# Expert results stored to places of their own and folded at the end, half of the shared tiles moved behind the expert steps

## The chip, the cores and the metric

One core of one Trainium2 chip runs one launch. The metric is device microseconds of that launch, the median of several runs. Names used: PE (TensorE), DVE (VectorE), ACT (ScalarE), POOL (GpSimd), SP (SyncE, here a queue that issues DMAs).

## The reference, cut to what matters

One transformer layer on 2048 tokens of 256 elements, float32. The second half is a mixture of experts with a shared expert:

```python
w, idx = _router(xf, rg_w, ru_w, extra_scale, extra_bias)     # top 4 of 16 experts per token
coeff = jnp.einsum('tk,tke->te', w, jax.nn.one_hot(idx, E, dtype=w.dtype))
def step(y, ew):
    wg, wu, wd, c = ew
    h = jax.nn.silu(xf @ wg.T) * (xf @ wu.T)                    # wg, wu: 176 x 256
    return (y + h @ wd.T * c[:, None], None)
y, _ = lax.scan(step, y0, (Wg, Wu, Wd, coeff.T))
z = jax.nn.silu(xf @ Sg.T) * (xf @ Su.T) @ Sd.T                 # shared expert, 352 wide
x = x + gb * (y + z)
```

## The kernel before

Three stages, each a block of its own with a barrier behind it: the projections with layernorm, sliding-window attention with routing, and the experts. Every matrix product is made of three float32r products of high and low parts (`three`, L109). Tokens are handled in 16 tiles of 128.

In the attention stage POOL's `weights` (L827) writes each token's 16 expert coefficients and its token number behind its row in `h2` (HW = 273 columns), and `dispatch` (L838) scatters the row to the four experts' regions of `xs_scr` in memory. The last pairs of tiles are dispatched behind the last attention work.

The expert stage is `experts_and_output` (L1208). Its first part runs the 16 shared tiles: per tile PE does gate and up (12 matmuls into both GU banks), the transposition XT of the tile after next, the shared down of two tiles before (YP) and the transposition HT of one tile before. PE's next gate and up waits for DVE's `gating` of this tile (L1557), which waits for ACT's `gate` (L1389). In the same tiles the 16 experts' weights are split, one a tile: ACT writes the high parts (`split_hi`, L1402), DVE the low part of gate and up (L1605, 128x704) and POOL the low part of down (L1470, 88x512). DVE also makes the table that says which rows and which expert each step has (L1508 to L1545), in tiles 0 to 3, in line with its work on the tiles; tile 5 on PE turns the table into a row. DVE adds the residual (`add_x1`) and SP stores each tile to out_x. POOL writes 128 neutral rows behind each expert's region (L1468).

The second part runs 80 steps of one expert and 128 gathered rows each, with gate and up (6 matmuls), XT of the step after next (2), down (6) of two steps before and HT (2) of one before. SP loads the rows four steps ahead (`load_x`, L1306), DVE scales the result by coefficient and gate (`y_gate`, L1569) into one of eight buffers (y_st and h2), and POOL adds it into out_x by an indirect DMA with an add in memory (L1488). The rows of one expert are different tokens, those of two experts may be the same: so `let_add` (L1316) on SP, in line with the loads, waits at an expert's first step until all adds before have landed, reading the count from the table, and lets POOL go on by `turn`.

Of the kernel before, what the change touches and what calls it, by code (L numbers as in the profile page):

```python
# [12 lines left out]
P = 128  # L13
# [31 lines left out]
SPARE = 5 * P  # L45
# [106 lines left out]
def project_qkv(nc, A, T, ctx, own):  # L152
# [87 lines left out]
    def _(eng):  # L240
# [18 lines left out]
        eng.dma_start(T["pad"][:, :], A["pad"]).then_inc(z_st, 16)  # L259
# [27 lines left out]
        eng.wait_ge(z_st, 32)  # L287
# [268 lines left out]
def attention_and_routing(nc, A, T, ctx, own):  # L556
# [41 lines left out]
    r_sm = sb("r_sm", [P, 3, 2])  # L598
    top8 = sb("top8", [P, 2, 8])
# [202 lines left out]
    def _(eng):  # L802
# [405 lines left out]
def experts_and_output(nc, A, T, out, ctx, own):  # L1208
# [18 lines left out]
    xs = T["xs_scr"]  # L1227
    NS = STEPS_RUN


    gu_hi = sb("gu_hi", [P, NE, W_GU], F32R)
# [5 lines left out]
    steps_c = sb("steps_c", [P, 4 + NE])  # L1237
    tab = sb("tab", [P, 8, NE])
    col = sb("col", [P, 8])
    entry_c = sb("entry_c", [P, 4])  # L1240
    pad_i = sb("pad_i", [P, NE], I32)
    step_i = sb("step_i", [1, 4, P], I32)
# [33 lines left out]
    x1_ld, o_out, added, turn = sems("x1_ld", 4), sems("o_out", 4), sems("added", 2), sem("turn")  # L1276
# [21 lines left out]

    @block.sync
    def _(eng):  # L1300
        def load_h2(n):
            if n >= 4:
                eng.wait_ge(xt_mm, n - 3)
            eng.dma_start(x_st[:, n % 4, 0:D], T["h2_scr"][n]).then_inc(xs_ld[n % 4], 16)

        def load_x(s, t):  # L1306

            eng.wait_ge(xt_mm, TILES + s - 3)
# [7 lines left out]
        def let_add(s):  # L1316

            for p in range(2):
                eng.wait_ge(added[p], step_entry(eng, 2 + p, s, 32 + 16 * NS))
                plain(eng)  # L1320
            eng.nop(nofuse=True).then_inc(turn, 1)  # L1321

        def load_x1(n):

            if n >= 4:
                eng.wait_ge(o_out[n % 4], 32 * (n // 4))
            eng.dma_start(y_st[:, n % 4, :], T["x1_scr"][n]).then_inc(x1_ld[n % 4], 16)

        def store_out(n):
            eng.wait_ge(y_out, n + 1)  # L1330
            for c in range(2):
                eng.dma_start(out[0:S_LEN, :].rearrange("(c n q) d -> n c q d", c=2, n=TILES)[n, c],
                              y_st[c * CH:(c + 1) * CH, n % 4, :]).then_inc(o_out[n % 4], 16)

        for n in range(2):
            load_h2(n)
        eng.dma_start(sgu_raw[:, :, :, :], A["sgu"]).then_inc(sgu_ld, 16)
        eng.dma_start(sdn_raw[:, :, :], A["sd"]).then_inc(sdn_ld, 16)
        for n in range(2, 4):
            load_h2(n)  # L1340
# [3 lines left out]
        for n in range(TILES):  # L1344
            if n < TILES - 4:
                load_h2(n + 4)
            else:
                if n == TILES - 4:
# [5 lines left out]
                load_x(n - (TILES - 4), n - (TILES - 4))  # L1354
            if n < TILES - 1:
                load_x1(n + 1)
            if n >= 2:
                store_out(n - 2)

        def step(s, r, i, first, last):  # L1360
            if runs(s, 0, NS - 5):
                load_x(s + 4, r % 4)
            if isinstance(s, int) and s < 2:
                store_out(TILES - 2 + s)
            if runs(s, 4):
                let_add(s - 4)

        for_steps(eng, step, NS)
        for s in range(NS - 4, NS):
            let_add(s)  # L1370
        for p in range(2):
            eng.wait_ge(added[p], 32 + 16 * (NS // 2))
# [4 lines left out]
    def _(eng):  # L1377
# [35 lines left out]
        for n in range(TILES):  # L1413
            gate(n, n % 2, GU[0], SH_I)
            x_hi(n + 2, n % 2)
            if n == 1:
# [5 lines left out]
            if n == 0:  # L1422
                eng.wait_ge(T["w_first"], 32 * FIRST)
            if n == FIRST:
                eng.wait_ge(w_rest, 64)
            split_hi(n)
# [417 lines left out]
```

## Time and profile before

| | |
|---|---|
| runs | 728.52, 722.45, 728.35 us; median 728.35 |
| profiled execution | 725.86 us, span 724.2 us |
| PE busy / weight loads / DVE / ACT / POOL | 77% / 72% / 55% / 39% / 41% |
| mean granted TensorE clock | 0.852 |
| shared tiles on PE | 403.8 to 486.75 us |
| first POOL subtract (L1470) | 409.8 us |
| expert steps on PE | 486.75 to 708.7 us |

A busy share is an average over stages with different limits; what a change in one stage is worth is read in that stage: what PE waits for, and what releases it. "idle before <-releaser" tells how long an engine stood before an instruction and what let it go. The clock is given as a share of 2.4 GHz: 1.00 or 0.50 when it does not change in a stretch.

### The profile page before, as it was taken

The page shows a single profiled execution, that of the slowest core. Times are in us where ns is not written, and L with a number is a line of the kernel's source. Part 1 is how long each engine was busy: PE and PEld are TensorE (multiplying, and loading weights), DVE is VectorE, ACT ScalarE, POOL GpSimd, SP SyncE. Part 2 cuts the span into 40 slices and gives each one's busy share as a digit, 9 for nine tenths or more (in the row PEclk, how much of TensorE's full clock was granted, in tenths as well). Part 3 has the DMA queues.
Part 4 walks back from the last instruction along what each step waited for, and adds up shares of the span by engine and source line. Part 5 has one row for each costly group of instructions (what it writes and reads, how often), then busy time and mean ns, then how long its engine had stood idle before and what let it go on. Part 6 is the DMA issues. An engine that isn't in the chain of part 4 may idle for free. (4 is left out here: it accounts for less than half of the span.)

```text
span 724.2 us, 14774 instructions
## 1 busy us (share of the span) xinstructions
PE 558.6 (77%) x3655; PEld 522.5 (72%) x3656; DVE 396.3 (55%) x1142; ACT 279.9 (39%) x739; POOL 300.5 (41%) x275
## 2 busy tenths in 40 slices
PE   2578841999988989889821489679895798789992
PEld 1378841898988989889720479679795697679892
DVE  3796420225456565575761677755673476357571
ACT  1334422224533343343310446354553354245450
POOL 3644405001014433352675334431463475465675
PEclk9799985559979889798955799899999999699997
DMA  7146694038835635531224936233463575476674
GB/s 209 39 138 193 172 263 124 11 110 207 197 80 148 163 100 144 145 110 62 92 99 169 320 94 187 66 85 72 83 109 66 84 127 88 67 119 103 105 113 51
DMA packets 73466, 88.93 MB, mean 123 GB/s; under 512 B 10122, under 2 KB 63369, under 8 KB 73345
## 3 DMA queue, kind: packets, MB, share of 16 engines
q1 hardware_dynamic: 53723, 58.93, 30.2%
q0 software_dynamic: 15712, 22.89, 17.5%
q10 hardware_dynamic: 3974, 6.47, 2.8%
q8 instruction: 21, 0.34, 0.2%
q14 instruction: 36, 0.29, 0.2%
HBM read 49.55 MB, written 39.66 MB: 123 GB/s over the span
## 5 line engine op out<-in xcount | busy, mean ns | idle before, releaser
L148 POOL DMA_INDIRECT xs_scr<-h,slot_u x64 | 62.4, 974 | 79.7 <-DVE slot_u L995 30.4
L113 PE MATMUL GU<-gu_hi,xT 128*128 x320 | 88.3, 359 | 4.7 <-POOL lo L1470 4.2
L1488 POOL DMA_INDIRECT out_x<-y_st,ids_st x40 | 62.3, 1558 | 66.3 <-SPq L1321 31.1
L1090 PE MATMUL O<-raw,prob 128*128 128x99 f32 (+1 forms) x512 | 80.8, 314 | 0.0
L1488 POOL DMA_INDIRECT out_x<-h,ids_st x40 | 62.2, 1554 | 40.6 <-issue 15.3
L760 ACT ACTIVATE prob<-TB 128x512 f32<-128x512 f32 x64 | 38.1, 596 | 103.3 <-PE TB L1080 76.8
L1090 PEld LDWEIGHTS O<-raw,prob 128*128 128x128 f32 x512 | 76.2, 229 | 0.4
L113 PE MATMUL YP<-dn_hi,aT 88*128 x320 | 70.1, 312 | 2.8 <-DVE aT L1554 2.5
L1630 PE MATMUL XT<-ident,x_st 128*128 128x128 f32 x192 | 40.2, 293 | 38.3 <-DMA x_st<-xs_scr 25.2
L1561 DVE TENSOR_TENSOR h_act<-GU,g_act 128x176 f32<-128x176 f32 (+1 forms) x96 | 35.7, 372 | 60.8 <-ACT g_act L1393 53.2
L1400 ACT ACTIVATE aT<-HT 88x256 fp32r<-88x256 f32 (+1 forms) x96 | 39.8, 415 | 75.4 <-PE HT L1640 69.1
L878 DVE TENSOR_REDUCE neg_m<-SB 128x4 f32<-128x512 f32 x64 | 43.0, 689 | 44.8 <-PE SB L1068 39.7
L1549 DVE TENSOR_TENSOR xT<-XT,xT 128x256 fp32r<-128x256 f32 x96 | 40.6, 423 | 40.8 <-ACT xT L1387 39.9
L1065 PE MATMUL SB<-mask_key,mask_qry 126*128 126x512 f32 x64 | 34.6, 541 | 35.7 <-POOL Q L811 24.3
L1630 PEld LDWEIGHTS XT<-ident,x_st 128*128 128x128 f32 x192 | 26.1, 147 | 47.5 <-DMA x_st<-xs_scr 31.2
L113 PEld LDWEIGHTS GU<-gu_hi,xT 128*128 128x128 f32 x320 | 55.2, 200 | 6.0 <-issue 5.9
L113 PEld LDWEIGHTS YP<-dn_hi,aT 88*128 88x128 f32 x320 | 50.4, 196 | 7.2 <-issue 4.1
L113 PE MATMUL GU<-lo,xT 128*128 x160 | 54.1, 338 | 0.0
L1387 ACT ACTIVATE xT<-XT 128x256 fp32r<-128x256 f32 x96 | 36.7, 382 | 44.8 <-PE XT L1630 43.6
L113 PE MATMUL GU<-sgu_hl,xT 128*128 128x352 f32 x192 | 37.7, 349 | 18.2 <-DVE h_act L1561 10.5
L1554 DVE TENSOR_TENSOR aT<-HT,aT 88x256 fp32r<-88x256 f32 (+1 forms) x96 | 44.5, 465 | 12.9 <-ACT aT L1400 9.4
L1393 ACT ACTIVATE g_act<-GU 128x176 f32<-128x176 f32 (+1 forms) x96 | 32.7, 341 | 46.3 <-PE GU L113 39.3
(192 smaller groups left out, 1270.1 us busy)
## 6 DMA issues: line engine op xcount, KB each, us to landing
x_st<-xs_scr SPq DMA_DIRECT2D x80, 136.5 KB, 2.3
K<-k_scr SPq DMA_DIRECT2D x48, 192.0 KB, 3.6
k_scr<-k_ev SPq DMA_DIRECT2D x8, 768.0 KB, 5.6
QC<-q_scr SPq DMA_DIRECT2D x24, 256.0 KB, 6.8
q_scr<-q_ev SPq DMA_DIRECT2D x8, 512.0 KB, 3.3
raw<-in_egu SPq DMA_DIRECT2D x8, 352.0 KB
raw<-in_egu ACTq DMA_DIRECT2D x2, 1408.0 KB
raw<-in_x SPq DMA_DIRECT2D x36, 64.0 KB, 3.0
```

What stands on the lines that cost most here:

```text
L113: mm = eng.matmul(out, a, b, start=(i + j == 0), stop=(i == len(pairs) - 1 and j == 2))
L148: eng.indirect_dma_start(T["xs_scr"], bass.IndirectOffsetOnAxis(ap=T["slot_u"][:, par, t % 2, k:k + 1], axis=0), T["h2"][:, t, :], None).t ...
L760: eng.activation(prob[:, q, :], TB[q % 2][:, :], ACT.Exp, scale=SCALE).then_inc(exp_done, 1)
L878: eng.tensor_reduce(neg_m[:, p2, 4 * q:4 * q + 4], SB[q % 2][:, :].rearrange("p (h x) -> p h x", h=4), AX.X, ALU.max, negate=True).then_in ...
L1090: mm = eng.matmul(O[:, head // 8, at:at + WIDE * VC], prob[:, q, hh * P:(hh + 1) * P], VW[:, bass.ds(HEADS * n + head, WIDE), :].rearrange ...
L1387: eng.activation(xT[:, p2, 0, :, :], XT[p2][:, 0:D].rearrange("p (k x) -> p k x", k=KD), ACT.Copy).then_inc(xT_hi2, 1)
L1400: eng.activation(aT[:, p2, 0, 0:k, :], HT[p2][0:FH, 0:k * P].rearrange("p (k x) -> p k x", k=k), ACT.Copy).then_inc(aT_hi, 1)
L1488: eng.indirect_dma_start(out, bass.IndirectOffsetOnAxis(ap=ids_st[:, r:r + 1].bitcast(U32), axis=0), results(r % 8), None, compute_op=ALU. ...
L1549: eng.tensor_tensor(xT[:, p2, 1, :, :], XT[p2][:, 0:D].rearrange("p (k x) -> p k x", k=KD), xT[:, p2, 0, :, :].bitcast(F32), ALU.subtract) ...
L1554: eng.tensor_tensor(aT[:, p2, 1, 0:k, :], HT[p2][0:FH, 0:k * P].rearrange("p (k x) -> p k x", k=k), aT[:, p2, 0, 0:k, :].bitcast(F32), ALU ...
L1561: eng.tensor_tensor(h_act[:, p2, 0:width], up, g_act[:, p2, 0:width], ALU.mult).then_inc(gated, 1)
L1630: mm = eng.transpose(XT[t % 2][:, k * P:(k + 1) * P], x_st[:, t, k * P:(k + 1) * P], ident[:, :])
```

## The change

- Routing: POOL's `weights` also works out for each chosen expert the place 4 x token + k, k being the rank of the expert among the token's four, and writes 16 such places behind the coefficients. HW is 288. Five more operations, and RP_OPS is 9.
- The first part runs 8 shared tiles (EARLY) and splits two experts a tile. ACT splits both, DVE subtracts the gate and up part of the even one, POOL that of the odd one and both down parts. Their sum with the residual goes back to `x1_scr`, not to out_x.
- The neutral rows are written by SP (`fill_up`), from an input array, in tile 3, with places of their own. The column with the expert's first step leaves the table.
- Steps: the result goes by an indirect DMA without an add to `ys_scr`, each row at its place. `let_add` and `turn` are gone. POOL waits, every second step, for sends of the step group before (`sent`).
- Behind the 80 steps the other 8 shared tiles run. Behind the last step's gate and up, `to_add`, `four` and `halves` lie where `gu_hi` lay: SP loads the 16 tiles of `x1_scr`, waits for all sends and loads `four`, a token's four results in 4 KB, two DMAs of 64 partitions a tile, six tiles ahead. POOL adds four into two and two into one, at most two tiles ahead of `final`. DVE adds the shared results of the late tiles (`add_late`) and then the fold (`finish`): tiles 0 to 3 among the late tiles, 4 to 15 behind the last shared result. SP stores to out_x.

```diff
 W_GU, W_DN = KD * 2 * FI, 2 * D
-TB_PAD, TB_COL = 9, 24
+TB_PAD, TB_COL = 9, 20
 L1_OPS, L2_OPS = 16, 16
-R_OPS, P_OPS, RP_OPS = 20, 4, 4
+R_OPS, P_OPS, RP_OPS = 20, 4, 9
 W_EXP = W_GU + W_DN
-HW = D + NE + 1
+HW = D + 2 * NE
...
+            k_of = [onehot[:, par, :, k, :] for k in range(TOPK)]
             eng.wait_ge(r_dve, R_OPS * g + R_OPS)
             c.mark(eng.tensor_tensor(rw[:, 0], rt[:, 7, :, :], esc[:, 0:1, :].broadcast_to([P, 2, NE]), ALU.mult)).wait(True)
             c.mark(eng.tensor_scalar(rw[:, 1], rw[:, 0], 1.0, None, ALU.add)).wait()
-            c.mark(eng.tensor_tensor(h2[:, 2 * par:2 * par + 2, D:IDS], mask_e[:, par].bitcast(F32), rw[:, 1], ALU.mult)).wait(True)
-            c.mark(eng.tensor_copy(h2[:, 2 * par:2 * par + 2, IDS:HW].rearrange("p a o -> p (a o)").bitcast(U32), T["ids"][:, bass.ds(n, 2)]))
+            c.mark(eng.tensor_tensor(h2[:, 2 * par:2 * par + 2, D:IDS], mask_e[:, par].bitcast(F32), rw[:, 1], ALU.mult))
+            c.mark(eng.tensor_tensor(pl[:, 0], k_of[1], k_of[3], ALU.add))
+            c.mark(eng.tensor_tensor(pl[:, 1], k_of[2], k_of[3], ALU.add)).wait(True)
+            c.mark(eng.tensor_tensor(pl[:, 2], pl[:, 0], T["ids"][:, bass.ds(n, 2)].unsqueeze(2).broadcast_to([P, 2, NE]), ALU.add)).wait()
+            c.mark(eng.tensor_tensor(pl[:, 0], pl[:, 2], pl[:, 1], ALU.add)).wait(True)
+            c.mark(eng.tensor_tensor(pl[:, 2], pl[:, 0], pl[:, 1], ALU.add)).wait(True)
+            c.mark(eng.tensor_copy(h2[:, 2 * par:2 * par + 2, IDS:HW].bitcast(U32), pl[:, 2]))
             assert c.k == RP_OPS
...
-        def let_add(s):
-
-            for p in range(2):
-                eng.wait_ge(added[p], step_entry(eng, 2 + p, s, 32 + 16 * NS))
-                plain(eng)
-            eng.nop(nofuse=True).then_inc(turn, 1)
...
+        def store_z(n):
...
+            eng.dma_start(T["x1_scr"][n], y_st[:, n % 4, :]).then_inc(z_out[n % 4], 16)
+
+        def fill_up():
+
+            eng.wait_ge(tb, TB_PAD)
+            for e in range(NE):
+                row = eng.value_load(pad_i[0:1, e:e + 1])
+                row = nc.s_assert_within(row, 0, NE * CAP, skip_runtime_bounds_check_because="a count of at most 2048 rows")
+                eng.dma_start(xs[bass.ds(row, P), :], A["pads"][e * P:(e + 1) * P, :]).then_inc(pad_st, 16)
...
+            if n == EARLY - 5:
+                fill_up()
...
-            if runs(s, 4):
-                let_add(s - 4)
+                store_z(EARLY - 2 + s)
...
+        eng.wait_ge(gu_mm, LATE)
+        for q in (2, 3, 0, 1):
+            if q == 0:
+                for t in range(4):
+                    eng.wait_ge(z_out[t], 16 * (EARLY // 4))
+            at = slice(4 * q, 4 * q + 4)
+            eng.dma_start(to_add[:, at, :], T["x1_scr"][at].rearrange("n p d -> p n d")).then_inc(add_ld[q], 16)
+            if q == 3:
+                for n in (EARLY + 4, EARLY + 5):
+                    load_h2(NS + n, n)
         for p in range(2):
-            eng.wait_ge(added[p], 32 + 16 * (NS // 2))
+            eng.wait_ge(sent[p], 32 + 16 * (NS // 2))
+
+        def load_four(n):
+            if n >= 6:
+                eng.wait_ge(folded, n - 5)
+            for c in range(2):
+                eng.dma_start(four[c * CH:(c + 1) * CH, n % 6].rearrange("p k d -> p (k d)"),
+                              halves_of(ys[0:PLACES, :].rearrange("(s k) d -> s (k d)", k=TOPK), n)[c]).then_inc(four_ld[n % 6], 16)
+
+        def store_out(n):
+            eng.wait_ge(final, n + 1)
+            for c in range(2):
+                eng.dma_start(halves_of(out, n)[c], y_st[c * CH:(c + 1) * CH, n % 4, :]).then_inc(o_out[n % 4], 16)
+
+        for n in range(6):
+            load_four(n)
+        for n in (EARLY + 6, EARLY + 7):
+            load_h2(NS + n, n)
+        for n in range(TILES):
+            store_out(n)
+            if n + 6 < TILES:
+                load_four(n + 6)
...
+        def dn_low(e):
             eng.wait_ge(w_hi2, 2 * e + 2)
             eng.tensor_tensor(lo[0:FH, e, W_GU:W_EXP], raw[0:FH, e, W_GU:W_EXP],
                               dn_hi[:, e, :].bitcast(F32), ALU.subtract).then_inc(dn_lo, 1)
 
-        eng.wait_ge(step_tab, 1)
-        for t in range(4):
-            eng.wait_ge(o_out[t], 32 * (TILES // 4))
+        for n in range(EARLY):
+            dn_low(2 * n)
+            eng.wait_ge(w_hi2, 4 * n + 3)
+            eng.tensor_tensor(lo[:, 2 * n + 1, 0:W_GU], raw[:, 2 * n + 1, 0:W_GU], gu_hi[:, 2 * n + 1, :].bitcast(F32),
+                              ALU.subtract).then_inc(dn_lo, 1)
+            dn_low(2 * n + 1)
+
         for p in range(2):
-            eng.wait_ge(added[p], 32)
+            eng.wait_ge(sent[p], 32)
 
         def step(s, r, i, first, last):
             q = r // 2 % 2
-            eng.wait_ge(turn, s + 1)
+            if r % 2 == 0 and runs(s, 4):
+
+                eng.wait_ge(sent[q], 32 * i + 32)
+                plain(eng)
+            eng.wait_ge(y_out, EARLY + s + 1)
             plain(eng)
-            if r % 2 == 0 and runs(s, 4):
-
-                eng.wait_ge(added[q], 32 * i + 32)
-            eng.wait_ge(y_out, TILES + s + 1)
-            plain(eng)
-            eng.indirect_dma_start(out, bass.IndirectOffsetOnAxis(ap=ids_st[:, r:r + 1].bitcast(U32), axis=0), results(r % 8), None,
-                                   compute_op=ALU.add).then_inc(added[q], 16)
+            eng.indirect_dma_start(ys, bass.IndirectOffsetOnAxis(ap=ids_st[:, r:r + 1].bitcast(U32), axis=0), results(r % 8),
+                                   None).then_inc(sent[q], 16)
 
         for_steps(eng, step, NS)
...
+        for n in range(TILES):
+            two = halves[:, n % 2]
+            eng.wait_ge(four_ld[n % 6], 32 * (n // 6) + 32)
+            if n >= 2:
+                eng.wait_ge(final, n - 1)
+            eng.tensor_tensor(two, four[:, n % 6, 0:2, :], four[:, n % 6, 2:4, :], ALU.add).then_inc(folded, 1)
+            eng.wait_ge(folded, n + 1)
+            eng.tensor_tensor(two[:, 0, :], two[:, 0, :], two[:, 1, :], ALU.add).then_inc(summed, 1)
...
+        def add_late(n):
+
+            eng.wait_ge(y_mm, NS + n + 1)
+            eng.wait_ge(add_ld[n // 4], 16)
+            eng.tensor_tensor(to_add[:, n, :], YP[n % 2][:, 0:D], to_add[:, n, :], ALU.add).then_inc(y_out, 1)
+
+        def finish(n):
+
+            eng.wait_ge(summed, n + 1)
+            if n < EARLY:
+                eng.wait_ge(add_ld[n // 4], 16)
+            elif n == EARLY:
+                eng.wait_ge(y_out, NS + TILES)
+            if n >= 4:
+                eng.wait_ge(o_out[n % 4], 32 * (n // 4))
+            eng.tensor_tensor(y_st[:, n % 4, :], halves[:, n % 2, 0, :], to_add[:, n, :], ALU.add).then_inc(final, 1)
...
+        for n in range(EARLY, TILES):
+            p2 = n % 2
+            gating(NS + n, p2, GU[1][:, 0:SH_I], SH_I)
+            if n < TILES - 2:
+                x_lo(NS + n + 2, p2)
+            if n < EARLY + 2:
+                s = NS + n - EARLY - 2
+                y_gate(s, s % UNROLL, s // 4)
+            else:
+                add_late(n - 2)
+            a_lo(NS + n - 1, 1 - p2, 2 if n == EARLY else 4)
+            for m in ((), (0,), (1,), (2, 3))[max(n - EARLY - 4, 0)]:
+                finish(m)
+        add_late(TILES - 2)
+        a_lo(NS + TILES - 1, 1, 4)
+        add_late(TILES - 1)
+        for n in range(4, TILES):
+            finish(n)
 
...
+        for n in range(EARLY, TILES):
+            w, p2 = NS + n, n % 2
+            shared_gate_up(w, p2)
+            if n < TILES - 2:
+                transpose_x(w + 2, (n + 2) % 4, (w + 2) // 4 + 1)
+            if n < EARLY + 2:
+                down(w - 2, p2, load_entry(w - 2 - EARLY))
+            else:
+                shared_down(w - 2, p2)
+            transpose_a(w - 1, 1 - p2, 2 if n == EARLY else 4)
+        transpose_a(NS + TILES - 1, 1, 4)
+        for w in (NS + TILES - 2, NS + TILES - 1):
+            shared_down(w, w % 2)
 
 
```

## Rows read from the trace of the kernel before

**Rows 1.** Windows: us, busy us of each engine (instructions), granted clock, DMA share, GB/s.
```profile
680.00:700.00 20.00, 20.00 (x146) 19.08 (x145) 14.52 (x37) 11.63 (x46) 14.82 (x10) 1.00 0.80 129
...
396.00:400.00 4.00, 0.69 (x2) 0.29 (x2) 0.42 (x1) 0.38 (x1) 3.08 (x4) 0.50 1.02 396
```

**Rows 2.** Waits of SP from 486 to 724: waited for, us in total, times, longest.
```profile
SPq L59 <- DMA out_x<-y_st,ids_st: 25.1, 9, 4.0
SPq L59 <- DMA out_x<-h,ids_st: 19.9, 7, 3.1
SPq L1374 <- DMA out_x<-h,ids_st: 11.8, 1, 11.8
```

**Rows 3.** Waits of PE from 486 to 724.
```profile
PE XT L1630 <- DMA x_st<-xs_scr: 25.2, 15, 3.0
```

**Rows 4.** Timeline of POOL: start, us, instruction, idle before and its releaser.
```profile
672.94 1.55 POOL L1488 DMA_INDIRECT out_x<-y_st,ids_st  x1 [3.59 <-DVE h L1577]
...
692.42 1.55 POOL L1488 DMA_INDIRECT out_x<-y_st,ids_st  x1 [0.47 <-issue]
```

**Rows 5.** Timeline of PE, gate and up of shared tiles and of steps 0 and 2.
```profile
446.65 2.16 PE L113 MATMUL GU<-sgu_hl,xT 128*128 128x352 f32 x12
...
450.64 2.17 PE L113 MATMUL GU<-sgu_hl,xT 128*128 128x352 f32 x12
...
460.37 3.86 PE L113 MATMUL GU<-sgu_hl,xT 128*128 128x352 f32 x12 [5.48 <-DVE h_act L1561]
...
466.37 2.17 PE L113 MATMUL GU<-sgu_hl,xT 128*128 128x352 f32 x12
...
486.75 0.95 PE L113 MATMUL GU<-gu_hi,xT 128*128 x2 [4.15 <-POOL lo L1470]
...
495.51 0.57 PE L113 MATMUL GU<-gu_hi,xT 128*128 x2
```

**Rows 6.** Timeline of POOL at the end of the attention stage.
```profile
371.49 0.19 POOL L835 COPY h<-ids 128x2 uint32<-128x2 uint32 x1
373.18 1.05 POOL L148 DMA_INDIRECT xs_scr<-h,slot_u  x1 [1.50 <-DVE slot_u L995]
...
384.31 0.19 POOL L835 COPY h<-ids 128x2 uint32<-128x2 uint32 x1
```

**Rows 7.** Timeline of ACT in a shared tile: the two splits.
```profile
447.43 0.78 ACT L1403 ACTIVATE gu_hi<-raw 128x704 fp32r<-128x704 f32 x1
448.11 0.62 ACT L1404 ACTIVATE dn_hi<-raw 88x512 fp32r<-88x512 f32 x1
```

**Rows 8.** A group (mean ns), and one line's min/median/max ns.
```profile
L819 POOL TENSOR_TENSOR h2t<-xn,mod 128x512 f32<-128x512 f32 x8 | 10.2, 1270 | 46.3 <-ACT xn L731 45.7 <-issue 0.6
...
L1605 DVE TENSOR_TENSOR lo<-raw,gu_hi x16: 874/892/7553, 412.8 to 483.9; 128x704 fp32r<-128x704 f32 x16
```

**Rows 9.** Timeline of POOL and of DVE in the shared tiles.
```profile
410.45 0.90 DVE L1510 TENSOR_TENSOR first_use<-count,steps_c 128x256 f32<-128x256 f32 x1 [1.32 <-DMA steps_c<-in_steps]
...
451.60 7.43 POOL L1470 TENSOR_TENSOR lo<-raw,dn_hi 88x512 fp32r<-88x512 f32 x6
...
452.23 7.55 DVE L1605 TENSOR_TENSOR lo<-raw,gu_hi 128x704 fp32r<-128x704 f32 x1
```

**Rows 10.** SP: the chain in order of time, and the timeline of SP's issues.
```profile
576.18 0.34 SPq L1314
576.66 0.27 SPq L1289
...
452.06 1.11 SPq L1332 DMA_DIRECT2D out_x<-y_st  x2
```

**Rows 11.** DMA issues: count, KB each, median us to landing.
```profile
x_st<-xs_scr SPq DMA_DIRECT2D x80, 136.5 KB, 2.3
...
xs_scr<-pad POOLq DMA_DIRECT2D x16, 136.5 KB, 2.9
...
out_x<-y_st SPq DMA_DIRECT2D x32, 64.0 KB, 2.1
```

More of the change, by code:

```diff
@@ L286, in _ @@
         eng.wait_ge(qk0_ld, 5 * LD)
-        eng.wait_ge(z_st, 32)
+        eng.wait_ge(z_st, 16)
     @block.scalar
@@ L1226, in experts_and_output @@
     ident, iota_e, count, gb, raw, lo, h2 = [T[x] for x in ("ident", "iota_e", "count", "gb", "raw", "lo", "h2")]
-    xs = T["xs_scr"]
+    xs, ys = T["xs_scr"], T["ys_scr"]
     NS = STEPS_RUN
+    LATE = NS + EARLY
+    with ExitStack() as last_use:
+        last = last_use.enter_context(nc.sbuf_tensor("last_use", [P, NE * W_GU], F32))
+    four = last[:, 0:6 * TOPK * D].rearrange("p (c k d) -> p c k d", c=6, k=TOPK)
+    to_add = last[:, 6 * TOPK * D:6 * TOPK * D + TILES * D].rearrange("p (n d) -> p n d", n=TILES)
+    halves = last[:, 6 * TOPK * D + TILES * D:6 * TOPK * D + TILES * D + 4 * D].rearrange("p (c k d) -> p c k d", c=2, k=2)
     gu_hi = sb("gu_hi", [P, NE, W_GU], F32R)
@@ L1275, in experts_and_output @@
     y_mm, y_out, picked = sem("y_mm"), sem("y_out"), sem("picked")
-    x1_ld, o_out, added, turn = sems("x1_ld", 4), sems("o_out", 4), sems("added", 2), sem("turn")
+    x1_ld, z_out, sent = sems("x1_ld", 4), sems("z_out", 4), sems("sent", 2)
+    four_ld, add_ld, folded, summed, final = sems("four_ld", 6), sems("add_ld", 4), sem("folded"), sem("summed"), sem("final")
+    o_out = sems("o_out", 4)
     block = ctx.enter_context(nc.Block())
@@ L1411, in _ @@
         eng.activation(sdn_hl[:, :, 0, :], sdn_raw[:, :, :], ACT.Copy).then_inc(sh_hi, 1)
-        for n in range(TILES):
+        for n in range(EARLY):
             gate(n, n % 2, GU[0], SH_I)
             x_hi(n + 2, n % 2)
+            if n == 0:
+                eng.wait_ge(T["w_first"], 32 * FIRST)
+            if 2 * n == FIRST:
+                eng.wait_ge(w_rest, 64)
+            split_hi(2 * n)
             if n == 1:
@@ L1454, in _ @@
             send_rows(eng, T, t, (GROUPS - 1) % 2)
-        half = P // 2
         for p in range(2):
-            eng.dma_start(out[S_LEN + p * half:S_LEN + (p + 1) * half, :], T["pad"][p * half:(p + 1) * half, 0:D]).then_inc(added[p], 16)
-            first = 2 * P * p
-            eng.dma_start(out[S_LEN + P + first:S_LEN + 3 * P + first, :], A["spare"][first:first + 2 * P, 0:D]).then_inc(added[p], 16)
-        for e in range(NE):
-            if e == 5:
-                eng.wait_ge(tb, TB_PAD)
-                with eng.Fori(0, NE // 4) as i:
-                    for j in range(4):
-                        row = eng.value_load(pad_i[0:1, bass.ds(4 * i + j, 1)], min_val=0, max_val=NE * CAP)
-                        eng.dma_start(xs[bass.ds(row, P), :], T["pad"][:, :]).then_inc(pad_st, 16)
+            for k in range(2):
+                first = PLACES + NE * P + (2 * p + k) * P
+                eng.dma_start(ys[first:first + P, :], A["pads"][0:P, 0:D]).then_inc(sent[p], 16)
+        def dn_low(e):
             eng.wait_ge(w_hi2, 2 * e + 2)
@@ L1525, in experts_of_steps @@
             c.mark(eng.tensor_scalar(row(5), cum, part, None, ALU.is_le)).wait()
-            c.mark(eng.tensor_reduce(col[:, 0:1], row(5), AX.X, ALU.add))
-            c.mark(eng.tensor_scalar(row(6), before, part, None, ALU.is_equal)).wait()
-            c.mark(eng.tensor_reduce(col[:, 1:2], row(6), AX.X, ALU.add))
+            c.mark(eng.tensor_reduce(col[:, 0:1], row(5), AX.X, ALU.add)).wait()
             c.mark(eng.tensor_scalar(row(7), e_row, col[:, 0:1], None, ALU.is_equal)).wait()
@@ L1590, in _ @@
                           ALU.subtract).then_inc(sh_lo, 1)
-        for n in range(TILES):
+        for n in range(EARLY):
             p2 = n % 2
-            if n == 5:
+            if n == EARLY // 2:
                 keep_steps()
```

149 lines of the change are left out of this document (70 added, 79 removed).

## Prediction

> **What bounds the kernel now.** I read the span in slices, then the last stage by PE's and SP's waits, by POOL's timeline and by windows, and last the stretch where the shared tiles run. The 80 expert steps run from 486.75 to about 708.7, which is 222 us or 2.78 a step. Undisturbed, a step is PE's: from 680 to 700 PE is busy throughout at full clock with 146 matmuls, 16 a step, so 2.19 us [rows 1]. The reader should see where the other 45 us go. SP stands 45.0 us in L59's table reads waiting for adds into out_x to land [rows 2]; SP is the engine that loads x_st, so PE stands 25.2 us for x_st [rows 3] and falls to half clock after some of the stops. POOL's timeline has two spacings: about 2.0 us inside an expert (0.47 idle, 1.55 issue), 5.1 at a change of expert (3.59 idle) [rows 4]. There are 15 such changes. So the steps are bound by PE plus the ordering of adds.
>
> The 16 shared tiles take 403.8 to 486.75. PE's period is 3.99 us (446.65 to 450.64), 6.0 at half clock (460.37 to 466.37) [rows 5]. Two stops matter: PE's 5.48 us before 460.37, and 4.15 before the first step, on POOL's last subtract.
>
> **The change, part by part** (times by the profiled execution, 724.2 span, 725.86 its own time, 1.7 around it; the median of the runs, 728.35, is 0.3% above that).
>
> *Routing, RP_OPS 4 to 9.* Five more operations on 32 columns, 0.25 each plus about 0.15 for each wait, the spacing in the rows: 1.85 us a pair. During attention POOL idles long before each dispatch, so it is hidden there. At the end it is not: the idle 1.50 before the send at 373.18 hides most of the first 1.85 (0.6 stays), and the last weights end the stage on POOL (384.31 + 0.19), +1.85 [rows 6]. **+2.4**. If hidden after all, 0.
>
> *Early stage, eight tiles.* PE needs 8 x 4.0 = 32. ACT splits two experts a tile: 0.68 + 0.75 by starts [rows 7], twice, plus 1.25 by starts for its gate, its copy of xT and its copy of aT is 4.1, no obstacle. POOL gets three subtracts a tile: 1.29 for 512 columns twice, and 128x704, not seen on POOL, by slope from 1.27 for 512 [rows 8] about 1.7: 4.25 a tile. So POOL runs almost without gap, and this is what I expect to decide. From 451.60 POOL ran six subtracts back to back for 7.43 us; DVE's subtract issued at 452.23, normally 0.89, lasted 7.55, to 459.8: it lost five changeovers in a row. Where POOL had a gap behind it, DVE's compare at 410.45 waited only for the one subtract then running, and lasted 0.90 [rows 8, 9]. Behind DVE's subtract the next tile's gating is queued, behind that PE, behind that ACT, and only when ACT has no more splits to give does POOL pause. Walked through: POOL's first run (six subtracts, experts 0 to 3) is 409.8 to 418.3; DVE's compare of 410.45 gets in at 418.3, then tables, subtract and gating, tile 2 on PE at 421.6, at half clock, tile 3 at 427.6. Second run 427.7 to 436.4; DVE then owes tables, two subtracts and the step table, tile 4 at 442.8, half clock again, tile 5 at 449.0. A shorter stop, tile 6 at 454.7. SP's 16 pad stores, moved from POOL, start behind the store of tile 1 at about 440.5; 0.27 read plus 0.35 to 0.6 issue each [rows 10] is 10 to 14 us, and landing 2.9 and the load 2.3 [rows 11] put XT of step 0 at about 459.8; tile 7 at 462.2. Last run to 471; steps start at 472.6 or 474.5 depending on ties. I take 473.5, with the 2.4 of above **475.9** instead of 486.75. If DVE always gets its turn after one POOL instruction, POOL's own 8 x 4.25 plus 8 x 0.89 behind 410 gives 451 + 2.4 = 453.4. These are the two ends; the single back-to-back case in the rows is the nearest, so the upper.
>
> The Trainium skill, page SBUF — State Buffer, section "SBUF: two separate sides", says that of a DVE instruction with two SBUF inputs and a GpSimd one, the first holds the shared ports for its whole length and the other blocks until it ends. Read as one instruction's wait, the early stage would be the 453.4 case; the row of 7.55 us shows six, so the trace disagrees with that reading.
>
> *Steps.* let_add and turn go, and with them the waits of 45.0. Sends are plain scatters, 1.05 or less [rows 6] instead of 1.55 [rows 4]. The wait on `sent` asks for sends three steps old, 6.6 us; plain stores land in 2.1 to 2.9 [rows 11]: hidden; were they to land later than that it would cost as before. The first two steps take 8.8 (486.75 to 495.51), they carry shared downs at half clock [rows 5]. 8.8 + 78 x 2.20 = 180.4, end at **656.3**; a saving of 41 of the 222.
>
> *Late stage, eight shared tiles.* Seven periods of 4.0 to the start of tile 15: 28. The loads of h2 for tiles 14 and 15 are queued on SP behind the wait for all sends and behind 12 loads of `four` (0.35 to 0.6 each, about 6.6), and behind their 3.1 MB, 8 us at the 396 GB/s of the weight loads [rows 1]; The last sends land about 7.5 us after tile 9 starts (2.0 of GU, 0.4 XT, 0.8 down, 0.5 gating, 1.0 send, 2.5 landing and a little between), so the h2 tile arrives at 17.5 where PE wants it at 14. **+4**, between 0 and 9. Tile 15 starts at 688.3.
>
> *The fold.* POOL may be only two tiles ahead of `final`, and DVE finishes tiles 0 to 3 before its last adds, so 12 finishes stand behind PE's end. A fold is 1.27 (512 columns) plus about 0.7 (256, by slope) plus 0.1 to 0.2 for its own wait: 2.1. DVE's finish has two SBUF inputs and finds POOL already in the next fold; it gets in at the gap between its two adds, 0.4 more on POOL: about 2.45. Finish 4 comes at 10.3 after tile 15 starts (GU, three downs, adds), finish 6 at 13.7, then nine more at 2.42: 35.5. **723.8**. Two stores are 1.1 of issue [rows 10] and 2.1 to land [rows 11]. In the kernel before the last landing ends SP's 11.8 us wait of about 707.4 [rows 2] and 5.0 follow to 724.2; the same again: **732.0**.
>
> *Nothing costed:* the smaller tables (four DVE operations fewer), rows of 1152 instead of 1092 bytes, one store instead of two in the early tiles: all beside PE.
>
> Sum: 724.2 + 2.4 - 13.3 (475.9 is 10.9 before 486.75, the 2.4 set apart) - 41.5 (steps) + 28 + 4 + 35.5 + 8.2 less the 15.5 now behind 708.7 = 732.0 span, 733.7 with the 1.7. By the median of the runs that is 0.7% more, by the profiled one 1.1%. I forecast **733**: the adds' 41 us are won and given back in the early stage and behind the last matmul. Own range 724 to 742.
>
> **The rivals.**
> 1. *DVE gets its turn between POOL's subtracts* (other side: faster). For it: only one back-to-back case is in the trace, and a wait met 0.1 us late lets DVE in. Steps start at 453.4 and the sum is 711. It decides once more than about three of the four long stops fall away. 0.32.
> 2. *The tail is shorter*: no wait for h2 (-4) and a fold at 2.1 (-3): 726. Against it: the order on SP. 0.10.
> 3. *The tail is bound by transfers or by SP.* Per tile 512 KB in and 128 KB out; at 396 GB/s 1.6 us, hidden. But each load spans 64 partitions; at 192 GB/s, half of it, 3.3, and ten tiles cost 9 more: 742. 0.08.
> 4. *The steps keep their stops*, in `sent` instead of `turn`: half the 41 back, 753. Against: no instruction waits for a landing younger than three steps. 0.05.
>
> The Trainium skill, page DMA: Bandwidth & Descriptors, section "Rules for kernel authors", says that transfers to disjoint partition halves use the same engines and serialize. Rival 3 would then be the plain 1.6 us and hidden; no row of the kernel before shows 4 KB rows over 64 partitions.
>
> **How the numbers follow.** Forecast 0.45. A measurement here can tell about 1% from no change. Of the forecast's 0.45, 0.03 lies more than 1% below the kernel before, 0.15 within 1%, 0.27 above. Rival 1 gives 0.30 faster, 0.02 same; rival 2 0.03, 0.06 and 0.01; rivals 3 and 4 0.13 slower. Faster 0.36, same 0.23, slower 0.41. The range reaches to rival 1 less 3 and beyond rival 3 by 2: 708 to 744.
>
> **What would show it.** Routing: the barrier after the attention stage some 2.4 us later. Early stage: DVE subtracts (the L1605 one) of several us while POOL's run on end, first step near 476; near 454 is rival 1. Steps: PE without waits for x_st after the first few, 180 us. Late: PE's wait for x_st at tile 14. Tail: PE idle some 33 us at the end, POOL and DVE alternating at 2.4. I am wrong if the DVE subtracts stay at 0.9 to 2.5 us, if the steps need over 190, or if the fold's period is off by 0.5.

## The result, and the profile after

The changed kernel takes 753.62 us (median of 4 runs, 750.5 to 755.93), the kernel before 728.31 (722.45 to 728.52): a ratio of 1.0365, interval 1.0299 to 1.0431. It is 3.65% slower. The prediction of 733, 708 to 744, was too low. Ratios, here and below, compare only undisturbed executions of both kernels on one chip, so they need not be the quotient of the medians. The profiled execution is 754.69, its span 752.8 against 724.2.

The span falls into stages that both traces mark. The forecast for each is worked out from the marks in the prediction (POOL's first send after the barrier, 390.43 before, stands at 392.83 with the routing's 2.4):

| stage | forecast | after | difference |
|---|---|---|---|
| up to POOL's first send after the barrier | 392.8 | 408.95 | +16.1 |
| early shared tiles, to the first step | 83.1 | 80.7 | -2.4 |
| 80 steps | 180.4 | 184.1 | +3.7 |
| late shared tiles, to the start of tile 15 | 32.0 | 39.4 | +7.4 |
| from there to the last finish | 35.5 | 32.4 | -3.1 |
| stores and the end | 8.2 | 7.35 | -0.85 |
| span | 732.0 | 752.8 | +20.8 |

Two stages hold the miss: attention, which the argument had passed by but for its last 2.4 us, and the late shared tiles.

**The steps did what was wanted.** Windows (columns as in [rows 1]) inside the steps, and PE's waits from 489 to 674:

```profile
580.00:600.00 20.00, 20.00 (x147) 19.28 (x146) 14.32 (x37) 11.77 (x46) 8.66 (x9) 1.00 0.43 126
600.00:620.00 20.00, 19.51 (x140) 18.18 (x138) 13.61 (x35) 11.47 (x45) 8.18 (x9) 1.00 0.40 124
```

```profile
PE GU L114 <- POOL lo L1523: 5.8, 1, 5.8
PE XT L1723 <- issue: 0.9, 4, 0.3
```

147 matmuls in 20 us are those of an undisturbed step before [rows 1], and the 25.2 us for x_st [rows 3] are gone: the only long wait is the one ahead of the first step. 222 us became 184. Not only SP's waits for adds went, but its table reads for them too (see "Steps" in the part on the prediction).

**Attention lost 16 us at one place.** DVE's timeline at tile 8, first in the kernel before, then in the changed one; windows around it, and the DMA queues from 244 to 256:

```profile
248.33 0.26 DVE L887 RECIPROCAL rden<-O 128x16 f32<-128x16 f32 x1 [0.56 <-issue]
```

```profile
253.66 0.26 DVE L894 RECIPROCAL rden<-O 128x16 f32<-128x16 f32 x1 [8.88 <-issue]
```

```profile
245.00:256.00 11.00, 2.50 (x18) 2.26 (x18) 2.24 (x5) 1.20 (x2) 3.97 (x4) 0.80 0.55 160
256.00:262.00 6.00, 6.00 (x27) 5.71 (x26) 2.23 (x4) 0.60 (x1) 0.00 (x0) 0.50 0.00 0
```

```profile
q14 instruction: 4, 0.03, 1.0%
```

"Issue" means that DVE waited for nothing that the profile shows. Tile 8 is the first behind the back branch of attention's loop (tiles 4 to 7, then 8 to 11). While DVE stands, PE does 2.5 us of work in 11, then runs at half clock (0.50) from 256 to 262, and q14, a queue that carries instructions, moves four packets. Between 230 and 260 of the kernel before q14 moves nothing, and DVE's idle before the same operation is 0.56. POOL's modulate, once a pair of tiles, shows the sum: 238.21 to 266.95 before (28.7), 233.94 to 277.88 after (43.9).

**Late tiles.** PE's timeline and SP's issues:

```profile
701.10 0.69 PE L1723 MATMUL XT<-ident,x_st 128*128 128x128 f32 x2 [10.43 <-DMA x_st<-h_scr]
704.85 2.55 PE L114 MATMUL GU<-sgu_hl,xT 128*128 128x352 f32 x12
```

```profile
684.24 8.40 SPq L1412 DMA_DIRECT2D last_use<-ys_scr  x12
692.68 1.06 SPq L1327 DMA_DIRECT2D x_st<-h_scr  x2
```

SP waits for all sends until 684.24, issues the 12 loads of `four`, then the two of h2, and the first lands 8.4 us later. PE wants it at 690.7, in tile 12.

**Early tiles and the fold.** Timelines of POOL and DVE in tile 1, POOL's in the fold, and DVE's finish as one line (min/median/max ns, first and last start):

```profile
431.17 2.93 POOL L1523 TENSOR_TENSOR lo<-raw,dn_hi 88x512 fp32r<-88x512 f32 x2
434.06 1.66 POOL L1529 TENSOR_TENSOR lo<-raw,gu_hi 128x704 fp32r<-128x704 f32 x1
```

```profile
432.57 0.41 DVE L1579 TENSOR_TENSOR first_use<-iota_e 128x256 f32<-128x256 f32 x1
433.01 2.99 DVE L1580 TENSOR_TENSOR first_use<-first_use,tab 128x256 f32<-128x256 f32 x1
```

```profile
728.23 1.26 POOL L1555 TENSOR_TENSOR last_use<-last_use 128x512 f32<-128x512 f32 x1
...
730.31 1.26 POOL L1555 TENSOR_TENSOR last_use<-last_use 128x512 f32<-128x512 f32 x1
```

```profile
L1657 DVE TENSOR_TENSOR y_st<-last_use x16: 409/1170/1470, 710.8 to 745.0; 128x256 f32<-128x256 f32 x16
```

DVE's operation at 433.01, 0.4 long when alone, took 2.99: it lost the changeover at 434.06 and got in at the next. None waited out a run of six as at 452.23 before [rows 9]; of DVE's eight subtracts the longest is 3.53 and the median 0.88. The fold's period is 2.08, and DVE's finish takes up to 1.47 instead of 0.41 without holding POOL.

### The profile page after: what moved, and what is told of

It reads as the page before. It is cut to its first block and busy times, and to the rows that moved or that the text cites. A ratio compares the mean times of both kernels' runs of the same rounds, so it can differ in the third digit from the quotient of the medians.

```text
span 752.8 us, 14319 instructions
## 1 busy us (share of the span) xinstructions
PE 564.6 (75%) x3651; PEld 532.6 (71%) x3652; DVE 405.2 (54%) x1146; ACT 280.1 (37%) x739; POOL 302.4 (40%) x338
## 5 line engine op out<-in xcount | busy, mean ns | idle before, releaser
L114 PE MATMUL GU<-gu_hi,xT 128*128 x320 | 84.9, 347 | 6.4 <-POOL lo L1523 5.8
L1097 PE MATMUL O<-raw,prob 128*128 128x99 f32 (+1 forms) x512 | 83.6, 321 | 0.0
L1097 PEld LDWEIGHTS O<-raw,prob 128*128 128x128 f32 x512 | 79.1, 236 | 0.2
L1544 POOL DMA_INDIRECT ys_scr<-y_st,ids_st x40 | 38.6, 964 | 64.5 <-DVE y_st L1639 64.5
L1723 PE MATMUL XT<-ident,x_st 128*128 128x128 f32 x192 | 38.6, 284 | 32.6 <-DMA x_st<-h_scr 25.2
L1544 POOL DMA_INDIRECT ys_scr<-h,ids_st x40 | 38.5, 962 | 52.4 <-DVE h L1639 51.1
L114 PEld LDWEIGHTS GU<-gu_hi,xT 128*128 128x128 f32 x320 | 52.4, 191 | 7.6 <-issue 7.6
L1075 PEld LDWEIGHTS SB<-K,Q 97*128 97x128 f32 x256 | 50.5, 245 | 4.1
L1723 PEld LDWEIGHTS XT<-ident,x_st 128*128 128x128 f32 x192 | 26.6, 144 | 37.1 <-DMA x_st<-h_scr 26.0
L1448 ACT ACTIVATE g_act<-GU 128x176 f32<-128x176 f32 (+1 forms) x96 | 32.8, 342 | 53.4 <-PE GU L114 50.3
L114 PE MATMUL GU<-sgu_hl,xT 128*128 128x352 f32 x192 | 40.5, 367 | 16.1 <-DVE h_act L1623 9.3
L114 PE MATMUL GU<-lo,xT 128*128 x160 | 52.0, 325 | 0.0
L1087 PEld LDWEIGHTS TB<-Q,K 97*128 97x128 f32 x256 | 48.9, 238 | 3.9
```

Source lines behind the costliest of these rows:

```text
L114: mm = eng.matmul(out, a, b, start=(i + j == 0), stop=(i == len(pairs) - 1 and j == 2))
L1075: mm = eng.matmul(bank[:, hh * P:(hh + 1) * P], queries(t, 4 * q + hh), keys(par, 4 * q + hh, j), start=False, stop=True, skip_group_check ...
L1087: mm = eng.matmul(bank[:, hh * P:(hh + 1) * P], keys(par, 4 * q + hh, j), queries(t, 4 * q + hh), start=False, stop=True, skip_group_check ...
L1097: mm = eng.matmul(O[:, head // 8, at:at + WIDE * VC], prob[:, q, hh * P:(hh + 1) * P], VW[:, bass.ds(HEADS * n + head, WIDE), :].rearrange ...
L1544: eng.indirect_dma_start(ys, bass.IndirectOffsetOnAxis(ap=ids_st[:, r:r + 1].bitcast(U32), axis=0), results(r % 8), None).then_inc(sent[q] ...
L1723: mm = eng.transpose(XT[t % 2][:, k * P:(k + 1) * P], x_st[:, t, k * P:(k + 1) * P], ident[:, :])
```

## The experiments

Each was timed beside the kernel before, on three chips where that ran at 720, 725 and 729 (medians). The changed kernel once more, as a measure:

> The changed kernel itself, on the chip of this comparison, as the measure for the others: expert stage entered near 409, steps from 490 to 674, last fold near 745, about 753, or as much less as this chip runs the kernel before faster.

750.2 us, ratio 1.0302 (1.0213 to 1.039). Entry (the table's first row, POOL's first send after the barrier) 403.5, early 82.7, steps 184.8, late 39.8, then 32.4 to the last finish, in the order of the table's stages. The entry differs by 5.4 from the first trace with the same code (9.61 idle at tile 8 again). All six traces that share this attention code enter between 399.7 and 409.0, 405.2 on average. So I compare stages, a single entry only with this spread of 9 in mind, and totals only with their interval.

### What holds DVE at tile 8

```
-        for_tiles(eng, tile)            # DVE, attention
+        for n in range(TILES):
+            tile(n, n % 4, n // 2, n // 4)
```

> The changed kernel, with the sixteen tiles of attention on DVE alone written out one after the other instead of a loop (same operations in the same order, no branch taken on DVE). In the changed kernel DVE's first operation of tile 8, behind the loop's back branch, stands 8.88 us idle with nothing to wait for, and the expert stage is entered at 408.95, 18.5 us later than before, where the routing accounts for 2.5. Theory (the branch on DVE costs the time, by its code's place or length): no idle of that kind near 254, expert stage entered near 393, time near 738. Rival (the five operations more on POOL, or their transfers, hold the attention up): entered near 409, time near 754. Rival (a disturbance of the one profiled execution): profile near 393 but the time still 754.

728.41 us, ratio 1.0211 (1.0094 to 1.0329). No such idle; DVE enters tile 8 at 239.21 with none. Entry 379.6, 29 us before the changed kernel's first trace and 24 before its second: more than the 16 that I wanted back. The two runs below that keep the loop and have no stall at tile 8 enter at 385.5 and 392.5, the three with the tiles written out (this one, a_all, a_all2) at 379.6 to 382.8: the loop seems to cost some us beside the stall, and no run shows where. POOL's operations were all there: that rival falls.

```
+        for _ in range(64):
+            eng.nop(nofuse=True).then_inc(shift, 1)
         for_tiles(eng, tile)            # DVE, attention
```

> The changed kernel with 64 empty instructions on DVE ahead of attention's loop, which move the loop's code without making it longer. If the 8.88 us idle on DVE at the back branch hangs on where the loop lies in the code, it changes or goes (expert stage entered near 393 plus what the 64 cost, at most 4); if it hangs on the loop's length (254 instructions where it was 252), it stays: entered at 409 to 413.

733.33 us (2 runs), entry 385.5. The loop is as long as in the changed kernel, lies 64 instructions further on, and the idle before tile 8's reciprocal is 0.46. So the loop's length alone doesn't decide. 5.29 us of the same kind turn up at 132.93, in the first tile.

```
             c.mark(eng.tensor_reduce(pk[...], ...)).wait()
+            if not isinstance(g, int):
+                plain(eng)              # before.py, DVE: twice in the loop's body
```

> The kernel before, with two empty instructions more in the body of attention's loop on DVE (254 instead of 252, as in the changed kernel), and the table reads of the waits for adds checked against bounds. Theory (two instructions more on DVE move the loop over a limit): 8 to 9 us idle on DVE before tile 8's reciprocal, first send of the last pair near 389 instead of 373, time near 744. Rival (it takes POOL's new operations): first send near 373, time 728 to 731.

```profile
254.25 0.26 DVE L887 RECIPROCAL rden<-O 128x16 f32<-128x16 f32 x1 [8.81 <-issue]
```

DVE's timeline of the kernel before with two empty instructions more: the stall is there, q14 moves its four packets between 240 and 256, and the expert stage is entered at 406.4 instead of 390.4, without one of the change's operations. The time, 781.45, is not attention's: with the bounds on SP's reads SP needs 2.7 us a step (its loads of x_st at 617.64 and 620.31), more than PE's 2.19, and PE stood 51.7 us for x_st in the steps [rows 3: 25.2].

```
-R_OPS, P_OPS, RP_OPS = 20, 4, 9
+R_OPS, P_OPS, RP_OPS = 20, 9, 9
-            c.mark(eng.tensor_copy(slot_u[...], ...))
+            eng.tensor_copy(slot_u[...], ...).then_inc(p_dve, P_OPS - c.k)
```

> The changed kernel with one instruction less in attention's loop on DVE (253; p_dve now counts by nine as r_pool does, so that both waits read one register). Theory (the loop with 254 lies over a limit, 252 within): if the limit is at 254 the idle of 8.9 us goes and the expert stage is entered near 393; if it is at 253, it stays, entered at 400 to 409. Either way the operations are the changed kernel's.

```profile
244.63 0.26 DVE L894 RECIPROCAL rden<-O 128x16 f32<-128x16 f32 x1 [0.57 <-issue]
```

736.0 us (2 runs, 741.37 and 730.63; the first is the profiled one, span 739.5). DVE's idle at tile 8 is 0.57, q14 moves nothing from 230 to 262 (27 packets in the whole span, the changed kernel 32), and the entry is 392.54 where I had forecast 392.83. This is the changed kernel with the same operations and one instruction less in the loop. Why the change had lengthened it: RP_OPS went from 4 to 9, so the threshold `RP_OPS * g + 1` that DVE waits for no longer has the value of `P_OPS * g + 1`; each of the loop's two uses then takes an instruction more, 254 in the built loop instead of 252.

```
-        for_tiles(eng, tile)            # before.py, DVE, attention
+        for n in range(TILES):
+            tile(n, n % 4, n // 2, n // 4)
```

> The kernel before, with attention's sixteen tiles written out on DVE as in a_unroll, and the read thresholds of SP's waits for adds held above zero by one register operation each. It gives the change's worth with no branch on DVE in either kernel. Theory (the branch cost the changed kernel 16 us and the kernel before nearly nothing): the first send of the last pair stays at 373 to 368, time within 1% of the kernel before, so that the change itself costs about 2% (728 against 720 on the chip of a_unroll). Rival (the kernel before pays at the branch too, in register work on DVE): last send 5 to 10 us earlier than 399.4, time 718 to 723, and the change itself costs 3%. Rival (the register operation on SP lengthens the steps as the bounded reads did in b_two): steps over 222 us.

739.41 us, ratio 1.0225 (1.0169 to 1.0282). Entry 385.4, 5.0 earlier than 390.4: less than the entries of one kernel differ, so whether the kernel before pays at its loop too stays open. The third thing expected happened: the register operation on SP lengthened the steps, PE stood 31.3 us for x_st, so the total says nothing of attention, and what the change is worth with no such loop on either side was not measured.

The stall is shown to be of DVE's loop, its code and where that lies, and to come with packets on the instruction queue. The exact limit is not shown: 252, 253 and 254 shifted by 64 run through, 254 in the old place does not. Nor is the length by itself the cause. In the kernel before, DVE's loop of the steps has 191 instructions as built, and at its back branch DVE stands 3.8 us while q14 moves three packets (640 to 650):

```profile
645.36 0.34 DVE L1561 TENSOR_TENSOR h_act<-GU,g_act 128x176 f32<-128x176 f32 x1 [3.81 <-issue]
```

In the changed kernel ACT's loop of the steps has 317, and from 560 to 660, over one of its turns, no instruction packet moves. The Trainium skill, page Runtime: NRT & Kernel Launch, section "Instruction fetch mechanics", has instructions fetched in blocks of 256 (16 KiB) and a taken branch to a block that is no longer held waiting for a fetch. Four packets of together 0.03 MB agree with two such blocks. When a block is given up the page doesn't say, so it doesn't tell a_pre64, which ran through, from the changed kernel.

### The late tiles

```
+        for n in (EARLY + 6, EARLY + 7):
+            load_h2(NS + n, n)
         for p in range(2):
             eng.wait_ge(sent[p], 32 + 16 * (NS // 2))
```

(and gone from behind the loads of `four`)

> The changed kernel with SP's loads of h2 for tiles 14 and 15 issued before its waits for the sends and the loads of the four results, instead of behind them. If their place on SP is why PE stands 10.43 us for x_st at 701.10: that idle goes, tile 13 starts near 693 instead of 704.85, and the time falls by 11 to 12.3, to about 742. Rival (the transfers compete: the loads of four take the engines whatever the order): the idle shrinks to 3 to 5 and the time falls by 5 to 7. Rival (the fold's chain on POOL and DVE sets the end): under 3 us.

735.85 us, ratio 1.0245 (1.0163 to 1.0327). The 10.43 idle is gone, tile 13 starts at 692.39, the late stage takes 26.7 instead of 39.4: 12.7 less, as the first theory had it. The ratio fell by less than that would be (1.0365 and 1.0302 to 1.0245), so the total alone would not have told this theory from the second. The traced execution is its longest, 741.9, but a_tail, with the same loads, has 26.6 in one of 731.75. In the trace SP issued the loads of `four` at 684.13, as before, and PE had no wait for x_st.

### The early tiles

```
-            eng.wait_ge(w_hi2, 4 * n + 3)      # POOL: the odd expert's 128x704
-            eng.tensor_tensor(lo[:, 2 * n + 1, 0:W_GU], ...)
+            for e in (2 * n, 2 * n + 1):       # DVE: both experts'
+                eng.tensor_tensor(lo[:, e, 0:W_GU], ...)
```

> The changed kernel with the odd experts' 128x704 subtracts on DVE instead of POOL, so that POOL has two subtracts of 512 columns a tile (2.6 us) and pauses, and DVE does 0.9 us more. Theory (in the early stage DVE's short table operations each wait for the POOL subtract that is running, and PE stands behind them): the early stage shrinks from 80.7 us to 60 to 70, steps start at 470 to 480 instead of 489.6, time 10 to 20 us under the changed kernel's on this chip. Rival (the 16 pad stores on SP and the load behind them set the end of the stage): the start of the steps moves by less than 5. Rival (DVE has no room for the subtracts): later than 490.

744.95 us, ratio 1.0251 (1.0138 to 1.0364), 5 under the changed kernel's 750.2; the intervals overlap, and the reading rests on the stage. Early stage 72.5 instead of 80.7 and 82.7: 8 to 10 less, with the same operations, one of POOL's three a tile moved to the engine that seemed behind. The stage missed the 60 to 70. DVE's operation at 432.24 is one of the few still held:

```profile
432.24 1.09 DVE L1581 TENSOR_TENSOR tab<-tab 128x16 f32<-128x16 f32 x1
```

What was left showed as 5.6 us for step 0's x_st behind the pad stores. Those, one tile earlier:

```
+            if n == EARLY - 6:
+                fill_up()
             if n >= 2:
                 store_z(n - 2)
-            if n == EARLY - 5:
-                fill_up()
```

> The changed kernel with the odd gate and up subtracts on DVE (a_lock) and SP's 16 pad stores one tile earlier, ahead of the store of tile 0 instead of behind the store of tile 1. In a_lock the stores ran from 39.2 to 54.8 us behind the stage's first send, step 0's x_st was transposed at 59.5 after 5.6 us idle, and the steps began at 72.5. Theory (the pad stores set when tile 6 goes on): stores from 27 to 43, no idle before that transposition, steps begin at 64 to 67. Rival (the last of POOL's subtracts sets it, idle 4.9 in a_lock): 70 to 72.

```profile
433.98 15.50 SPq L1355 DMA_DIRECT2D xs_scr<-in_pads  x16
```

```profile
471.37 0.95 PE L114 MATMUL GU<-gu_hi,xT 128*128 x2 [4.87 <-POOL lo L1523]
```

SP's and PE's timelines: the stores 29 to 45 us behind the first send, no idle ahead of step 0's transposition, and the steps begin at 66.5, inside the 64 to 67. 733.88 us, ratio 1.0115 (1.0078 to 1.0152). The pad stores' 15.5 us were the second bound. What is left is the third: PE's 4.87 us for POOL's last subtract.

### The fold

```
-            two = halves[:, n % 2]
+            two = four[:, n % 6, 0:2, :]       # POOL, no wait for final
-                eng.wait_ge(folded, n - 5)     # SP, load_four
+                eng.wait_ge(final, n - 5)
```

(with a_h2's order)

> The changed kernel with h2 of tiles 14 and 15 loaded before the waits for the sends (as in a_h2) and with POOL's sums left in place in four, so that POOL may run six tiles ahead of DVE's finish instead of two. With the loads alone POOL stood 4.2, 1.7, 1.7 and 0.8 us for a finish and its last fold ended at 732.2, tile 15 having started at 700.2. Theory (POOL's allowance of two tiles costs what it waits there): last fold 8 us earlier, near 724, time near 744 less what this chip runs faster, 20 under the changed kernel. Rival (SP's issues set the pace: 16 pairs of stores and 10 pairs of loads at 1.24 us a pair from 690 on end at 722 and the fold follows): 726 to 730. Rival (the 256 KB loads land in 4 us and hold POOL): no gain over a_h2, 13 under the changed kernel.

739.0 us, ratio 1.0175 (1.0081 to 1.0268), 11 under 750.2 and not 20. Late stage 26.6 again, but from tile 15's start to the last finish 32.8, a_h2's was 32.45. POOL began its sixth fold as tile 15 started (690.36 and 689.75), where in a_h2 it had folded two, and gained nothing. Timelines of SP and POOL:

```profile
704.86 1.23 SPq L1414 DMA_DIRECT2D last_use<-ys_scr  x2
706.14 1.23 SPq L1420 DMA_DIRECT2D out_x<-y_st  x2
```

```profile
707.11 1.26 POOL L1553 TENSOR_TENSOR last_use<-last_use 128x512 f32<-128x512 f32 x1 [0.71 <-DMA last_use<-ys_scr]
...
709.74 1.26 POOL L1553 TENSOR_TENSOR last_use<-last_use 128x512 f32<-128x512 f32 x1 [0.51 <-DMA last_use<-ys_scr]
```

A pair of stores and a pair of loads are 2.55 us of SP, back to back, and POOL's period is now 2.6 behind them. A wait of one kind gave way to one of another; my favourite theory fell.

### Together

> The changed kernel with all of it: attention's tiles written out on DVE, all gate and up subtracts on DVE, h2 of tiles 14 and 15 loaded early, sums in place, and the stores of tiles 4 to 15 issued by ACT. If the separate gains add up (26 us for attention's entry less what the copy costs, 10 to 20 early, 13 for the loads, 8 for the folds, 0 to 5 for the stores): a span of 680 to 695, under the kernel before by 3 to 6%. If they hide one another: 700 or more.

710.21 us, ratio 0.9763 (0.9683 to 0.9843): entry 379.8, early 73.9, steps 184.8, late 26.7, then 31.0 and 7.25. Span 703.5, above the 680 to 695: the folds gave 1.4 us, not 8 and more, though ACT now issued twelve of the sixteen pairs of stores. So SP's issues were not alone in holding the fold; POOL still waits 0.2 to 0.5 us for most loads.

> a_all (703.5 span, 4% under the changed kernel's chip mate) with the earlier pad stores of a_fill, DVE's finishes of tiles 0 to 6 spread over shared tiles 12 to 15 instead of 0 to 3 over 13 to 15, and SP storing tiles 0 to 7. In a_all POOL's folds ran at 2.04 and waited 0.2 to 2.6 each for loads that wait for finishes. Expected: early stage 74 to 66, tail 31.0 to 26 with 1 to 2 us more in the shared tiles: span about 692, ratio 0.96 to the kernel before. If POOL's lock makes the earlier finishes long (1.5 each) PE is held up as much as the tail gains: 696.

697.18 us, ratio 0.9583 (0.9533 to 0.9634), 4.2% faster than the kernel before. Early 67.2, from tile 15's start 27.7, near the 66 and 26. The span of 696.1 is the number named for long finishes, and they are long (up to 1.51), but PE was not held up: the late stage takes 26.6, as in a_all. What keeps the span above 692 is an entry 3.0 later than a_all's, 1.2 in the early stage and 1.7 in the tail. (The text above sets a_all 4% under the changed kernel; by the spans, 703.5 to 750.6, it is 6%.)

## Why the prediction was wrong, and where it was right

**Routing, +2.4: right in itself.** From the last modulate to the end of the weights the stage takes 19.72 us after and 17.26 before, 2.46 more. That the entry of a_short came within 0.3 us of the forecast is in part luck: a_pre64, also without the stall at tile 8, enters 7.3 earlier than forecast.

**The step that failed: attention costed at nothing.** The sentence "during attention POOL idles long before each dispatch, so it is hidden there" is true, and no answer to what happened. I counted what the edit adds on POOL and never what it does to DVE, whose source lines in attention are the same; two thresholds that no longer share a register made its loop two instructions longer. DVE stood 8.9 us at the back branch and PE ran at half clock behind it: 16.1 of the 20.8 us missed, and the same 16.0 that b_two adds to the kernel before. Single entries differ, but the averages say the same: 405.2 over the six traces of the changed kernel's attention code, 389.0 over a_short and a_pre64. With one instruction less the kernel takes 741.37 and 730.63 us, inside the forecast's own range of 724 to 742, with a ratio of 1.0156 (1.0070 to 1.0241) against the 1.007 forecast. That it is so near is partly luck, since the other stages missed by -2.4, +3.7, +7.4, -3.1 and -0.85 and cancel down to 4.7.

**Late stage, +4: the mechanism right, the size wrong.** I named the two loads behind the sends and `four`, and gave them 0 to 9. Counted from tile 9's start (677.08), SP woke at 7.2 (7.5 forecast) and PE wanted the tile at 13.6 (14). But SP issued for 8.4, 0.70 each, instead of 6.6, and the load landed 8.4 behind its issue, with the 12 others ahead of it, instead of about 3: at 24.0, not 17.5. So the failed terms are SP's price of a load and the landing behind twelve others. A wait of 10.4 instead of 4, and 1 us of slower clock behind it, are the 7.4. a_h2 shows the whole of it, 12.7.

**Early stage, 83.1 against 80.7: the sum right, a part of its reason wrong.** POOL did run nearly without gap, its new subtract took 1.66 (1.7 taken), and taking it from POOL gave back 8 to 10 us. But DVE did not lose whole runs, one of the signs that I had named for being wrong. It lost one changeover at a time and many times, at its short table operations. Tiles 4 to 6 were 4 to 7 us earlier than walked, and the pad stores gave most of it back: step 0's x_st came only 3.3 earlier. Rival 1, DVE always in its turn, would have been 453.4; even a_fill, with more room on POOL, needs 66.5 us against its 60.6 from entry. The Trainium skill, page SBUF — State Buffer, section "SBUF: two separate sides", lets a blocked instruction wait for the one that holds the ports. This trace, with none or one changeover lost, is nearer to that than to the row of six.

**Steps, 180.4 against 184.1.** Rival 4 didn't happen; that its 753 is the measured time is chance. "PE plus the ordering of adds" left out a part of what bound the steps before: SP's own instructions. Where SP waited for nothing it issued x_st at 571.18 and 573.22 (the chain of the kernel before), 2.04 us apart, so against PE's 2.19 it could hardly catch up after a wait. The change takes let_add's reads away with its waits: SP's loop has 173 instructions as built, before 341. In b_two and b_unroll SP's waits for adds were 41.0 and 42.6 us, no more than the 45.0 before, and the steps got longer all the same. How the 38 us won divide between landings and SP's reads is not shown. The 20 us windows in which PE repeats the steps' loop (near 555 and 611) hold 140 matmuls instead of 147, about 1 us each; with smaller losses where it enters and leaves it (near 505 and 664) that is most of the 3.7. The instruction queues move nothing from 560 to 660, so it isn't the stall of attention.

**Fold, 35.5 against 32.4.** The period is 2.08, not 2.45: DVE's finish waits for POOL and costs POOL nothing. Rival 2 had the fold's period, and lost its other half to h2. Rival 3's pace was near (its 192 GB/s should read 198, half of 396; the 3.3 stands) but not its reason: SP's issues alone need 2.55 a tile (a_tail), while a load of 256 KB lands in 4.3 with several under way.

**What the chances missed.** All rivals were stages that the change names. None was a stage that it leaves alone, and the range had no room for one.

## What to carry to other kernels

When an edit changes a constant of a loop's waits, compare the built loops of all engines, the untouched ones too, and look first at the stages that should not move: a stage that moved is found in one look at its marks. Where an engine stands "<-issue" at the first instruction behind a back branch, with packets on an instruction queue, try the loop shorter, moved or written out before anything else is tuned; its length alone did not tell here (191 stalled, 317 did not). On the queue that a stage depends on, put what is wanted first ahead of waits that it doesn't need, and ask for when the consumer reads ahead, not when it computes.

## What the runs showed of the hardware

- Two instructions more in a loop of 252 on DVE: 8.8 to 10.4 us of stand-still at its back branch in seven traces, and some 16 us of stage, with the clock at 0.50 for some us after it. The same loop 64 instructions further on did not stall at that branch (0.46).
- A loop of 191 instructions on DVE stood 3.8 us at its back branch once, in the one trace of the kernel before (645.36).
- DVE against POOL: one lost changeover per instruction is usual for those that meet a POOL subtract (0.4 becomes 1.1 to 3.0); waiting out a run of six [rows 9] was not seen again in the changed kernel.
- Indirect stores of 128 rows without the add are issued in 0.96 us (median of 80), 1.55 with it [rows 4].
- A step's table reads, waits and load took SP 2.04 us in the kernel before and 2.7 in b_two where it waited for nothing.
- SP's issue of 64 partitions by 4 KB takes 0.62 to 0.70 us each, so that 26 pairs keep SP busy through a tail of 512 KB in and 128 KB out a tile (a_tail).
